# Attention and expert kernel on one core: Newton step of the norms moved to GpSimd, a layer norm's last step to ScalarE, and a new order of the calls

## Chip, cores and metric

One core of a Trainium2 chip. The time is the device time of one execution of the whole kernel in microseconds; the median of the runs counts, lower is better.

## What is computed

32 blocks of 128 tokens with 256 features each, and a context of the same shape. First a cross attention per block with 16 heads of 16 columns, whose scores are not divided by a constant but by the squared sum of the lengths of query and key:

```python
x = x + xattn(layernorm(x), ctx, ctx)
    # scores = alpha * 4 * (q.k) / (|q| + |k|)**2, softmax, times v, times Wo + bo
x = x + ffn(layernorm(x))
    # router softmax over 8 experts, best 2, weights renormalised
    # expert: gelu(x @ W1 + b1) @ W2 + b2, hidden size 1024
```

`layernorm(x) = (x - mean) / sqrt(var + 1e-5)`, without a learned scale.

## The kernel before, in words

**Two stages.** The attention stage works on 16 pairs of blocks (`NP`, index p or `it`, with b = 0 or 1 for the block in the pair). In it, the router picks two experts per token and scatters each token's record to a table in HBM, and the expert weights are split into two f16 halves, one matrix a pair. The expert stage (from L714 on) runs 71 slots of 128 records through the experts' two products and adds the results to the output. It is not touched by the change.

**Order.** Each engine has one instruction stream, written by hand-ordered calls: a loop over `it` with one call per step, each for pair it+2 down to it-3 (L328 SyncE, L589 TensorE, L873 ScalarE, L1270 VectorE, L1498 GpSimd). Nothing else orders the work but semaphores: an engine that waits in one call holds all calls behind it. In PSUM, scores (`s_ps`), factors (`u_ps`) and attention values (`pv_ps`) have places of their own, once each; 32 other uses a pair share three banks `gen` in a fixed cyclic order, the list `TURNS`. A use waits until the use three places earlier has been read.

**One pair's way through the attention stage.**
1. `means` (VectorE, L1048 to L1050): statistics of the input block. `norm` (GpSimd): the power -0.5 of the variance (L1435), then (x - mean) * rstd on 128x256 (L1439), into `xn`. TensorE transposes it (L404), ScalarE copies it out (L779, `x_turned`).
2. `project` (TensorE, L413 to L422): query, key and value. ScalarE `squares` (L794, L797) and `v_out` (L786). VectorE `squares` (L1067): the squared lengths `n2` of the 32 query and key heads of each block. ScalarE `roots`: y = exp(-0.5 ln n2) (L806, L808).
3. `norms` (VectorE, L1072 to L1087): one Newton step that makes the lengths exact, and their split into three bf16 parts in `ar`. TensorE `rows` (L433) transposes them; VectorE `rows` (L1095, L1098) copies them out; six DMAs of the SyncE queue (L307, `flat_rows`) lay them flat into `uk`.
4. GpSimd `units` (L1482, L1485) scales query and key; TensorE `stack` (L452, L459) transposes them, ScalarE `stack` (L814, L817) copies them out.
5. For n = 0 to 3 (block n // 2, half of the heads n % 2): TensorE `factors` (L474) sums the lengths by one matmul, ScalarE `factors` takes ln and exp of -2 times it (L825, L827). TensorE `scores` (L486); VectorE `scores`: product `tw` (L1108) and maxima `tm` (L1113). GpSimd `split_max`: for even n the maxima as two bf16 (L1466, L1468), for odd n subtracted from all scores (L1461). TensorE `turned` (L496, L504) transposes and, for even n, subtracts the maxima; ScalarE `turned` (L835) takes the exponential; TensorE `values` (L521).
6. `heads_out`, `heads_back`, `turn_on`, `o_turned`, `project_out`, `residual` (L842, L529, L1120, L1124, L536, L848, L543, L546, L1135): division by the sum, output projection and residual, stored by SyncE. Then the second layer norm `norm_again` (L1447, L1453), `turn_y` (L553), `record_high` and `record_low` (L855, L859, L1473), `logits` (L560, L1143).
7. Routing, for four blocks together, so every second pair: `choose`, `counts` in one iteration, `route_exp`, `shares` (L1178 on), `ranks` (L566), `positions` (L1200 to L1210) in another, then eight scatters from GpSimd (L1495). In pair 11's `positions` a table of the first 20 slots is made (`soon_tables`, L1230 on; its last row is that of L1227).
8. Weights: `weight_products` (L581), `weight_sum`, their exponent on VectorE, `weight_high` (ScalarE, L870), `weight_low` (VectorE, L1258).

The lines that the change moves to GpSimd:

```python
step(dve.tensor_tensor(na["y2"][:, :, :], na["y"][:, :, :], na["y"][:, :, :], ALU.mult))
step(dve.scalar_tensor_tensor(na["n2y2"][:, :, :], n2[:, :, :], TINY, na["y2"][:, :, :],
                              ALU.max, ALU.mult))
```

Of the kernel before, what the change touches and what calls it, by code (L numbers as in the profile page):

```python
# [78 lines left out]
def build(nc, ctx, io):  # L79
# [119 lines left out]
    with ExitStack() as a:  # L199
# [26 lines left out]
        norm_bufs = {"ln": stats(a, "ln")}  # L226
        qk = alloc(a, "qk", [P, 2, 2 * NH, DK], F32)
# [5 lines left out]
              for k in ("ln", "y", "y2", "n2y2", "rn", "r1", "r2")}  # L233
# [36 lines left out]
        def sync_program(sp):  # L270
# [57 lines left out]
            for it in range(-4, NP + 1):  # L328
                if 0 <= it < NP:
                    load_weights(it)  # L330
                if NE <= it - 1 < NP - 1:
                    store_w2(it - 1)
                if 0 <= it + 1 < NP:
                    flat_rows(it + 1)
# [4 lines left out]
                if 0 <= it < NP:  # L339
                    residual(1, it)  # L340
                if 2 <= it + 3 < NP:
                    load(1, it + 3)
                if 0 <= it - 1 < NP - 1:
                    store_x1(1, it - 1)
                if 2 <= it + 4 < NP:
                    load(0, it + 4)
                if it == -4:
# [49 lines left out]
        def tensor_program(pe):  # L397
# [191 lines left out]
            for it in range(-1, NP + 3):  # L589
                if 0 <= it - 2 < NP - 1:  # L590
                    logits(0, it - 2)
                if 0 <= it < NP:
                    stack(0, it)
                if 0 <= it - 1 < NP:
                    values(1, it - 1)
                    turned(2, 0, it - 1)
                if 0 <= it + 1 < NP:
                    norm(1, it + 1)
                if 0 <= it - 1 < NP:
                    weight_products(it - 1)  # L600
                    heads_back(0, it - 1)
                if 0 <= it - 2 < NP - 1:
                    turn_y(1, it - 2)
                if 0 <= it < NP:
                    factors(0, it)
                if 0 <= it - 2 < NP - 1:
                    logits(1, it - 2)
                if 0 <= it - 1 < NP:
                    weight_sum(it - 1)
                    turned(2, 1, it - 1)  # L610
                    turn_on(0, it - 1)
                if 0 <= it < NP:
                    scores(0, it)
                    stack(1, it)
                if 0 <= it - 3 < NP - 1 and it % 2 == 0:
                    ranks(it - 3)
                if 0 <= it < NP:
                    factors(1, it)
                if 0 <= it - 1 < NP - 1:
                    project_out(0, it - 1)  # L620
                if 0 <= it - 1 < NP:
                    turned(3, 0, it - 1)
                    values(2, it - 1)
                    turned(3, 1, it - 1)
# [990 lines left out]
```

## Time and profile before

| | us |
|---|---|
| median of 3 runs | 940.22 |
| lowest, highest | 936.03, 941.43 |
| the profiled execution's own time | 935.94 |
| its span, first to last instruction | 934.1 |
| TensorE, VectorE, ScalarE, GpSimd busy | 873.3, 686.2, 595.9, 450.2 |
| mean granted TensorE clock | 0.978 of full |

PE is TensorE, PEld its weight loads, DVE VectorE, ACT ScalarE, POOL GpSimd. Times in a timeline are microseconds from the span's start. "[0.28 <-DVE ar L1087]" behind a row says that the engine stood idle for 0.28 us before it and was released by that instruction. A busy time of TensorE holds modelled ends, so that neighbouring rows overlap; the distance from start to start says how long a group really holds the engine.

### The profile page before, as it was taken

To read this page: it belongs to the slowest core of one execution; us is meant where nothing else is said; L and a number is where in the kernel's file an instruction comes from. 1 tells how busy PE (TensorE), PEld (TensorE's weight loads), DVE (VectorE), ACT (ScalarE), POOL (GpSimd) and SP (SyncE) were. 2 spreads that over 40 slices of the span, in tenths; PEclk is the share of its full clock that TensorE was granted. 3 is DMA by queue.
4 is the path that set the end of the run, shared out by engine and by line. 5 is a ranking of instruction groups with operands and counts; after the bars stand their busy time and mean duration, and the time that the engine had idled before them with its cause. 6 is when DMAs were issued, how large, how long until landed. Compare 5 with 4: busy or idle time off the path is not lost.

```text
span 934.1 us, 29246 instructions
## 1 busy us (share of the span) xinstructions
PE 873.3 (93%) x10189; PEld 757.7 (81%) x10189; DVE 686.2 (73%) x1671; ACT 595.9 (64%) x1204; POOL 450.2 (48%) x508
## 2 busy tenths in 40 slices
PE   3899999999999999999887899999999999999994
PEld 2677887777777877777665798999999999999993
DVE  6677888888888888888767478666666666666662
ACT  2588887877878878788564464455555555555551
POOL 7445576758666586675554425323222322223222
PEclk9899999999999999999889899999999999999997
DMA  5212322223231453242344933432332323333322
GB/s 157 69 44 74 93 93 87 68 90 128 76 104 60 137 173 121 88 152 84 121 138 134 413 80 74 99 69 49 51 51 48 54 48 53 48 54 50 46 27 22
DMA packets 61885, 84.72 MB, mean 91 GB/s; under 512 B 9872, under 2 KB 55312, under 8 KB 59568
## 3 DMA queue, kind: packets, MB, share of 16 engines
q1 hardware_dynamic: 47504, 64.26, 21.8%
q0 software_dynamic: 13296, 18.00, 11.6%
q8 instruction: 86, 1.41, 0.6%
q10 hardware_dynamic: 944, 0.60, 0.2%
q14 instruction: 55, 0.45, 0.2%
HBM read 49.86 MB, written 31.92 MB: 88 GB/s over the span
## 4 chain that ended last, share of the span: by engine, by line
PE 75%; DVE 11%; issue 7%; ACT 2%; POOL 2%; DMA 1%; SPq 0%; DVEq 0%; POOLq 0%; ACTq 0%
PE s_ps L714 11%; PE pv_ps L732 10%; PE u_ps L714 10%; PE gen L732 10%; PE s_ps L486 5%; PE gen L496 4%; PE pv_ps L521 3%; PE gen L546 2%; PE gen L459 2%; PE gen L560 2%; PE u_ps L474 2%; PE gen L683 2%; PE gen L504 2%; PE gen L581 1%; DVE tw L1108 1%
## 5 line engine op out<-in xcount | busy, mean ns | idle before, releaser
L1542 POOL DMA_INDIRECT out<-yw,rb x71 | 110.4, 1554 | 268.3 <-DVE yw L1367 243.0
L937 ACT ACTIVATE h<-s_ps,b1t,inv 128x128 f32<-128x128 f32 x288 | 107.3, 458 | 89.6 <-PE s_ps L714 86.2
L937 ACT ACTIVATE h<-u_ps,b1t,inv 128x128 f32<-128x128 f32 x280 | 104.2, 460 | 87.2 <-PE u_ps L714 86.9
L1350 DVE TENSOR_SCALAR hs<-h,hsc 128x512 f16<-128x512 f32 x142 | 70.4, 496 | 120.5 <-ACT h L937 78.9
L835 ACT ACTIVATE pt<-gen,escale 128x512 f32<-128x512 f32 x128 | 87.0, 681 | 44.3 <-PE gen L504 35.4
L1352 DVE SCALAR_TENSOR_TENSOR hs<-h,hsc,hs 128x512 f16<-128x512 f32 x142 | 106.7, 751 | 5.1
L714 PE MATMUL s_ps<-xt,w1s 128*128 128x128 f16 x1728 | 105.3, 221 | 2.6 <-issue 2.5
L714 PEld LDWEIGHTS s_ps<-xt,w1s 128*128 x1728 | 100.4, 99 | 3.5 <-issue 3.0
L1495 POOL DMA_INDIRECT xrec<-rec,idx x64 | 72.3, 1129 | 62.3 <-DVE idx L1210 47.0
L714 PE MATMUL u_ps<-xt,w1s 128*128 128x128 f16 x1680 | 100.7, 219 | 1.4 <-issue 1.4
L732 PE MATMUL pv_ps<-w2s_sb,hs 128*128 x864 | 100.5, 272 | 0.9 <-issue 0.9
L714 PEld LDWEIGHTS u_ps<-xt,w1s 128*128 x1680 | 95.8, 98 | 2.1 <-issue 1.8
L732 PE MATMUL gen<-w2s_sb,hs 128*128 x840 | 97.4, 273 | 0.0
L1108 DVE TENSOR_TENSOR tw<-th,s_ps 128x1024 f32<-128x1024 f32 x64 | 77.8, 1216 | 21.9 <-PE s_ps L486 15.0
L732 PEld LDWEIGHTS pv_ps<-w2s_sb,hs 128*128 128x128 f16 x864 | 82.4, 98 | 11.2 <-issue 1.8
L732 PEld LDWEIGHTS gen<-w2s_sb,hs 128*128 128x128 f16 x840 | 80.8, 98 | 8.8
L496 PE MATMUL gen<-idf,tw 128*128 128x128 f32 x512 | 80.8, 281 | 1.3 <-ACT pt L835 0.6
L1113 DVE TENSOR_REDUCE tm<-tw 128x8 f32<-128x1024 f32 x64 | 78.1, 1220 | 2.2
L486 PE MATMUL s_ps<-kt,qt 32*128 32x128 f32 x1024 | 76.0, 287 | 0.7 <-DVE tw L1108 0.6
L1461 POOL TENSOR_TENSOR tw<-tw,tm 128x1024 f32<-128x1024 f32 x32 | 60.7, 1896 | 31.1 <-DVE tm L1113 31.1
L486 PEld LDWEIGHTS s_ps<-kt,qt 32*128 32x128 f32 x1024 | 63.6, 190 | 13.4 <-issue 11.8
L496 PEld LDWEIGHTS gen<-idf,tw 128*128 128x128 f32 x512 | 60.9, 145 | 15.9 <-issue 10.5
(241 smaller groups left out, 1684.0 us busy)
## 6 DMA issues: line engine op xcount, KB each, us to landing
wl<-L_ffn_W SPq DMA_DIRECT2D x16, 1024.0 KB
rb<-xrec SPq DMA_DIRECT2D x71, 132.5 KB
w2s<-wst SPq DMA_DIRECT2D x8, 1024.0 KB, 8.8
w2s_sb<-w2s SPq DMA_DIRECT2D x8, 1024.0 KB, 19.5
xin<-x SPq DMA_DIRECT2D x32, 128.0 KB, 2.1
cin<-ctx SPq DMA_DIRECT2D x32, 128.0 KB, 2.3
xres<-x SPq DMA_DIRECT2D x32, 128.0 KB, 2.5
out<-x SPq DMA_DIRECT2D x30, 128.0 KB, 2.1
```

Source lines behind the costliest of these rows:

```text
L486: ins = pe.matmul(s_ps[:, i, j * P:(j + 1) * P], qt[b][rws, j // 2, :], kt[b][rws, j // 2, j % 2, :], start=True, stop=True)
L496: ins = pe.matmul(g[:, j * P:(j + 1) * P], tw[h][:, i, j, :], idf[:, :], is_transpose=True, start=(j == 0), stop=(h == 1 and j == 3))
L714: ins = pe.matmul(hbank[n % HBANKS][:, o:o + SLOT], w, xt[s % 2][:, xp, k, :], start=(t == 0), stop=(t == len(terms) - 1))
L732: ins = pe.matmul(y, hs[s % 3][:, hp, m, :], w, start=(m == 0 and t == 0), stop=(m == HC - 1 and t == 2))
L835: act.activation(pt[n % 2][:, i, :], turn(f"ex{n}{i}", p)[:, :], ACT.Exp, scale=escale[:, :]).then_inc(sig(f"ex{n}{i}"), 1)
L937: ins = act.activation(h32[n % HBANKS][:, m % HB, :], hbank[n % HBANKS][:, o:o + SLOT], ACT.Gelu, scale=inv1[:, bass.ds(ex, 1)].bitcast(F3 ...
L1108: dve.tensor_tensor(tw[h][:, :, :, :].rearrange("p i j k -> p (i j k)"), th[h][:, :], s_ps[:, :, :].rearrange("p i k -> p (i k)"), ALU.mul ...
L1113: dve.tensor_reduce(tm[h][:, :], tw[h][:, :, :, :].rearrange("p i j k -> p (i j) k"), AX.X, ALU.max).then_inc(sig(f"tm{n}"), 1)
L1350: dve.tensor_scalar(hi, h, scale, None, ALU.mult).then_inc(sig("hi"), 1)
L1352: dve.scalar_tensor_tensor(lo, h, scale, hi, ALU.mult, ALU.subtract).then_inc(sig("lo"), 1)
L1495: pool.indirect_dma_start(xrec_d[:, :], bass.IndirectOffsetOnAxis(ap=idx[:, i, t:t + 1], axis=0), rec[m % 2][:, t, :], None).then_inc(sig( ...
L1542: pool.indirect_dma_start(out[:, :], bass.IndirectOffsetOnAxis(ap=rb[j][:, D + NE:D + NE + 1], axis=0), yw[s % 2][:, :], None, compute_op= ...
```

## The change

Five things change.

`norms` goes from VectorE's list to GpSimd's. There the steps with two operations on three operands are written as two instructions, or once for all (`n2c`), so nine become eleven. The layer norm's GpSimd part makes only a column `minus_mean` = -mean * rstd; ScalarE then writes `xn` by one activation with scale and bias. `TURNS` and the five lists of calls are put in a new order.

```diff
-    ("lg0", -2, "rl_0", None), ("qte0", 0, "qte0", None), ("kte0", 0, "kte0", None), ("ex20", -1, "ex20", None),
-    ("xct1", 1, "xce1", None), ("wgr", -1, "wdg", None), ("ob0", -1, "on", 0), ("xu1", -2, "xue", 1),
-    ("lg1", -2, "rl_1", None), ("wsum", -1, "wcl", None), ("ex21", -1, "ex21", None), ("oc0", -1, "ote", 0),
-    ("qte1", 0, "qte1", None), ("kte1", 0, "kte1", None), ("rank", -3, "rpos", None), ("wo0", -1, "x10", None),
-    ("ex30", -1, "ex30", None), ("ex31", -1, "ex31", None), ("qk1", 1, "qke1", None), ("v1", 1, "ve1", None),
-    ("xct0", 1, "xce0", None), ("qk0", 1, "qke0", None), ("v0", 1, "ve0", None), ("ex00", 0, "ex00", None),
-    ("ex01", 0, "ex01", None), ("ob1", -1, "on", 1), ("ex10", 0, "ex10", None), ("rows_t", 1, "rowq", None),
-    ("oc1", -1, "ote", 1), ("ex11", 0, "ex11", None), ("xu0", -1, "xue", 0), ("wo1", -1, "x11", None),
+    ("wo1", -2, "x11", None), ("ex10", -1, "ex10", None), ("ex11", -1, "ex11", None), ("ex20", -1, "ex20", None),
+    ("qte1", 0, "qte1", None), ("kte1", 0, "kte1", None), ("ex21", -1, "ex21", None), ("rows_t", 0, "rowq", None),
+    ("wgr", -1, "wdg", None), ("xu0", -2, "xue", 0), ("wsum", -1, "wcl", None), ("xu1", -2, "xue", 1),
+    ("lg0", -2, "rl_0", None), ("ob0", -1, "on", 0), ("lg1", -2, "rl_1", None), ("xct1", 1, "xce1", None),
+    ("xct0", 1, "xce0", None), ("ex30", -1, "ex30", None), ("rank", -3, "rpos", None), ("ex31", -1, "ex31", None),
+    ("qk1", 1, "qke1", None), ("v1", 1, "ve1", None), ("qk0", 1, "qke0", None), ("v0", 1, "ve0", None),
+    ("oc0", -1, "ote", 0), ("ob1", -1, "on", 1), ("ex00", 0, "ex00", None), ("wo0", -1, "x10", None),
+    ("oc1", -1, "ote", 1), ("ex01", 0, "ex01", None), ("qte0", 1, "qte0", None), ("kte0", 1, "kte0", None),
...
+        minus_mean = pair(a, "minus_mean", [P, 1], F32)
...
-              for k in ("ln", "y", "y2", "n2y2", "rn", "r1", "r2")}
+              for k in ("ln", "y", "n2c", "y2", "n2y2", "rn", "r1", "r2")}
...
+            def normed(b, p):
+                act.wait_ge(*at(f"sh{b}", p + 1))
+                if p:
+                    act.wait_ge(*at(f"xct{b}", p))
+                act.activation(xn[b][:, :], xin[b][:, :], ACT.Identity, bias=minus_mean[b][:, :],
+                               scale=norm_bufs["ln"][b][3][:, :]).then_inc(sig(f"xn{b}"), 1)
...
-            def norms(p):
-
-                dve.wait_ge(*at("ny", p + 1))
-                step(dve.tensor_tensor(na["y2"][:, :, :], na["y"][:, :, :], na["y"][:, :, :], ALU.mult))
-                step(dve.scalar_tensor_tensor(na["n2y2"][:, :, :], n2[:, :, :], TINY, na["y2"][:, :, :],
-                                              ALU.max, ALU.mult))
-                step(dve.scalar_tensor_tensor(na["rn"][:, :, :], na["n2y2"][:, :, :], -3.0, na["y"][:, :, :],
-                                              ALU.add, ALU.mult))
-                step(dve.scalar_tensor_tensor(na["r1"][:, :, :], n2[:, :, :], TINY, na["rn"][:, :, :],
-                                              ALU.max, ALU.mult))
-                if p:
-                    dve.wait_ge(*at("rows_t", p))
-                part = lambda i: ar[:, :, :, i * STRIP:i * STRIP + NH]
-                v4 = lambda t: t[:, :, :].rearrange("p b (i h) -> p b i h", h=NH)
-                step(dve.tensor_copy(part(0), v4(na["r1"])))
-                step(dve.tensor_tensor(v4(na["r2"]), v4(na["r1"]), part(0), ALU.subtract))
-                step(dve.tensor_copy(part(1), v4(na["r2"])))
-                step(dve.tensor_tensor(v4(na["r1"]), v4(na["r2"]), part(1), ALU.subtract))
-                dve.tensor_copy(part(2), v4(na["r1"])).then_inc(sig("parts"), 1)
...
+            steps = 0
+
+            def step(ins):
+                nonlocal steps
+                steps += 1
+                ins.then_inc(sig("pool_own"), 1)
+                pool.wait_ge(sig("pool_own"), steps)
...
             def norm(b, p):
                 _, mv, var, rstd = norm_bufs["ln"][b]
                 pool.wait_ge(*at(f"ln{b}ve", p + 1))
+                if p:
+                    pool.wait_ge(*at(f"xn{b}", p))
                 pool.tensor_tensor(rstd[:, :], var[:, :], mhalf[:, :], ALU.pow).then_inc(sig(f"ln{b}rs"), 1)
                 pool.wait_ge(*at(f"ln{b}rs", p + 1))
-                if p:
-                    pool.wait_ge(*at(f"xct{b}", p))
-                pool.tensor_scalar(xn[b][:, :], xin[b][:, :], mv[:, 0:1], rstd[:, :], ALU.subtract,
-                                   ALU.mult).then_inc(sig(f"xn{b}"), 1)
+                pool.tensor_scalar(minus_mean[b][:, :], rstd[:, :], mv[:, 0:1], -1.0, ALU.mult,
+                                   ALU.mult).then_inc(sig(f"sh{b}"), 1)
...
+            def norms(p):
+
+                for b in range(2):
+                    pool.wait_ge(*at(f"n2{b}", p + 1))
+                step(pool.tensor_scalar(na["n2c"][:, :, :], n2[:, :, :], TINY, None, ALU.max))
+                pool.wait_ge(*at("ny", p + 1))
+                step(pool.tensor_tensor(na["y2"][:, :, :], na["y"][:, :, :], na["y"][:, :, :], ALU.mult))
+                step(pool.tensor_tensor(na["n2y2"][:, :, :], na["n2c"][:, :, :], na["y2"][:, :, :], ALU.mult))
+                step(pool.tensor_scalar(na["n2y2"][:, :, :], na["n2y2"][:, :, :], -3.0, None, ALU.add))
+                step(pool.tensor_tensor(na["rn"][:, :, :], na["n2y2"][:, :, :], na["y"][:, :, :], ALU.mult))
+                step(pool.tensor_tensor(na["r1"][:, :, :], na["n2c"][:, :, :], na["rn"][:, :, :], ALU.mult))
+                if p:
+                    pool.wait_ge(*at("rows_t", p))
+                part = lambda i: ar[:, :, :, i * STRIP:i * STRIP + NH]
+                v4 = lambda t: t[:, :, :].rearrange("p b (i h) -> p b i h", h=NH)
+                step(pool.tensor_copy(part(0), v4(na["r1"])))
+                step(pool.tensor_tensor(v4(na["r2"]), v4(na["r1"]), part(0), ALU.subtract))
+                step(pool.tensor_copy(part(1), v4(na["r2"])))
+                step(pool.tensor_tensor(v4(na["r1"]), v4(na["r2"]), part(1), ALU.subtract))
+                pool.tensor_copy(part(2), v4(na["r1"])).then_inc(sig("parts"), 1)
...
```

The lists, one iteration each (numbers in brackets are n or b; n,i for `turned`; the offset of the pair against `it` where it is not 0):

TensorE before: logits(0) -2, stack(0), values(1) -1, turned(2,0) -1, norm(1) +1, weight_products -1, heads_back(0) -1, turn_y(1) -2, factors(0), logits(1) -2, weight_sum -1, turned(2,1) -1, turn_on(0) -1, scores(0), stack(1), ranks -3, factors(1), project_out(0) -1, turned(3,0) -1, values(2) -1, turned(3,1) -1, project(1) +1, factors(2), values(3) -1, norm(0) +1, scores(1), project(0) +1, turned(0,0), scores(2), factors(3), turned(0,1), heads_back(1) -1, turned(1,0), rows +1, values(0), turn_on(1) -1, turned(1,1), turn_y(0) -1, project_out(1) -1, scores(3).

TensorE after: factors(3) -1, project_out(1) -2, turned(1,0) -1, turned(1,1) -1, scores(3) -1, values(0) -1, turned(2,0) -1, stack(1), turned(2,1) -1, rows, weight_products -1, turn_y(0) -2, values(1) -1, weight_sum -1, turn_y(1) -2, logits(0) -2, heads_back(0) -1, values(2) -1, logits(1) -2, norm(1) +1, norm(0) +1, scores(0), turned(3,0) -1, ranks -3, turned(3,1) -1, factors(0), project(1) +1, values(3) -1, factors(1), project(0) +1, scores(1), turn_on(0) -1, factors(2), heads_back(1) -1, turned(0,0), project_out(0) -1, scores(2), turn_on(1) -1, turned(0,1), stack(0) +1.

ScalarE after: turned(1,0) -1, normed(1) +1, turned(1,1) -1, turned(2,0) -1, stack(1), turned(2,1) -1, record_high(0) -2, heads_out(0) -1, record_high(1) -2, weight_high -1, x_turned(0) +1, x_turned(1) +1, normed(0) +2, turned(3,0) -1, turned(3,1) -1, factors(0), squares(1) +1, v_out(1) +1, factors(1), route_exp -2, squares(0) +1, heads_out(1) -1, v_out(0) +1, o_turned(0) -1, factors(2), turned(0,0), roots +1, o_turned(1) -1, turned(0,1), stack(0) +1, factors(3).

VectorE before: scores(1) -1, squares(1), squares(0), means(1) +1, norms, heads_back(1) -2, rows, scores(2) -1, residual(1) -2, logits(0) -2, scores(3) -1, weight_diagonal -1, heads_back(0) -1, means(0) +2, logits(1) -2, weight_exponent -1, shares and positions -3 (even it) or choose and counts -2 (odd it), residual(0) -1, weight_low -1, scores(0).

VectorE after: scores(1) -1, heads_back(1) -2, squares(0), residual(0) -2, scores(2) -1, residual(1) -2, scores(3) -1, means(0) +2, rows, weight_diagonal -1, weight_exponent -1, logits(0) -2, heads_back(0) -1, logits(1) -2, shares and positions -3 (even it) or choose -2 (odd it), weight_low -1, counts -2 (odd it), means(1) +2, scores(0), squares(1) +1.

GpSimd after: norm(1) +2, record_low(0) -2, units(1) +1, split_max(0), units(0) +1, split_max(1), norms +1, split_max(2), norm_again(0) -1, norm_again(1) -1, norm(0) +3, split_max(3), five scatters -3 (even it), record_low(1) -1, three scatters -2 (odd it). Before, three scatters of -4 (odd it) or three of -3 (even it) stood behind split_max(3), and two of -3 (even it) behind split_max(1).

SyncE after: flat_rows, store_w2 -1, load(0) +3, load_weights, load(1) +3, residual(1), store_x1(1) -1, residual(0), store_x1(0) -1. Before: load_weights, store_w2 -1, flat_rows +1, residual(0), store_x1(0) -1, residual(1), load(1) +3, store_x1(1) -1, load(0) +4.

The calls behind the attention loop, among them the last pair's output projection and routing, are as before.

## Rows read from the trace of the kernel before

**Rows 1.** Page, part 1: busy us (share of the span) xinstructions.

```profile
PE 873.3 (93%) x10189; PEld 757.7 (81%) x10189; DVE 686.2 (73%) x1671; ACT 595.9 (64%) x1204; POOL 450.2 (48%) x508
```

**Rows 2.** Timeline of PE: start us, us, engine line op; weight products, first expert product.

```profile
51.01 1.08 PE L581 MATMUL gen<-wl 128*128 128x128 bf16 x16
...
137.03 1.08 PE L581 MATMUL gen<-wl 128*128 128x128 bf16 x16
...
432.94 1.08 PE L581 MATMUL gen<-wl 128*128 128x128 bf16 x16
...
469.19 1.08 PE L581 MATMUL gen<-wl 128*128 128x128 bf16 x16
...
517.01 4.58 PE L714 MATMUL s_ps<-xt,w1s 128*128 128x128 f16 x48 [2.51 <-issue]
```

**Rows 3.** Windows: stretch, length, busy PE PEld DVE ACT POOL, clock, DMA, GB/s.

```profile
80.00:110.00 30.00, 29.58 (x311) 24.15 (x308) 23.11 (x52) 24.20 (x42) 18.14 (x23) 1.00 0.27 82
...
137.00:433.00 296.00, 288.26 (x2994) 232.56 (x2993) 256.70 (x671) 237.27 (x396) 204.17 (x261) 1.00 0.34 109
...
440.00:500.00 60.00, 52.37 (x503) 41.35 (x502) 44.09 (x108) 37.80 (x58) 30.60 (x37) 0.86 0.33 109
```

**Rows 4.** Timeline of PE inside one pair.

```profile
305.40 0.60 PE L496 MATMUL gen<-idf,tw 128*128 128x128 f32 x4
305.84 0.61 PE L504 MATMUL gen<-negb,mhl 128*128 128x128 bf16 x8
...
306.73 0.60 PE L496 MATMUL gen<-idf,tw 128*128 128x128 f32 x4
307.62 0.42 PE L433 MATMUL gen<-idb,ar 128*96 128x128 bf16 x4 [0.28 <-DVE ar L1087]
```

**Rows 5.** Waits, 137 to 433 us: engine line <- releaser: us, times, longest.

```profile
POOL xrec L1495 <- DVE idx L1210: 30.0, 5, 6.1
ACT pt L835 <- PE gen L504: 20.5, 26, 1.6
...
PE gen L433 <- DVE ar L1087: 3.5, 10, 0.4
...
PE gen L504 <- POOL mhl L1468: 1.8, 5, 0.4
```

**Rows 6.** Timeline of DVE: first of the nine norm instructions, one inside, the row behind.

```profile
304.61 0.22 DVE L1072 TENSOR_TENSOR na_y<-na_y 128x64 f32<-128x64 f32 x1
...
306.74 0.59 DVE L1086 TENSOR_TENSOR na_r<-na_r,ar 128x64 f32<-128x64 f32 x1
...
307.48 0.25 DVE L1120 RECIPROCAL rz<-gen 128x16 f32<-128x16 f32 x1
```

**Rows 7.** Groups of POOL: busy us, mean ns of one; idle before.

```profile
L1439 POOL TENSOR_SCALAR xn<-xin,ln_mv,ln_rstd 128x256 f32<-128x256 f32 x32 | 40.5, 1264 | 12.7 <-PE gen L404 10.0
...
L1482 POOL TENSOR_TENSOR qu<-qk,colscale 128x256 f32<-128x256 f32 x32 | 19.7, 616 | 0.0
...
L1466 POOL CAST mhl<-tm 128x8 bf16<-128x8 f32 x32 | 6.0, 188 | 30.3 <-DVE tm L1113 30.3
```

**Rows 8.** Groups of ACT.

```profile
L855 ACT ACTIVATE rec<-xn 128x256 f16<-128x256 f32 x32 | 13.3, 416 | 0.0
```

**Rows 9.** Timeline of PE: behind the early tables, and in the last pair.

```profile
446.43 0.59 PE L413 MATMUL gen<-bqp,ones_b 96*128 96x512 bf16 x1 [4.02 <-DVE x L1135]
...
480.82 0.60 PE L474 MATMUL u_ps<-uk,aq 99*128 99x512 bf16 x2 [1.99 <-ACT th L825]
```

**Rows 10.** Timeline of PE at the start.

```profile
24.23 0.66 PE L433 MATMUL gen<-idb,ar 128*96 128x128 bf16 x4 [4.25 <-DVE ar L1087]
```

**Rows 11.** Timelines of DVE and POOL.

```profile
87.98 2.34 DVE L1258 SCALAR_TENSOR_TENSOR w1s<-wl,wsc,w1s 128x2048 f16<-128x2048 f32 x1
...
88.14 2.60 POOL L1447 TENSOR_TENSOR lm_rstd<-lm_var,mhalf 128x1 f32<-128x1 f32 x1 [6.48 <-DVE lm_var L1050]
```

**Rows 12.** Groups of POOL: scatters.

```profile
L1495 POOL DMA_INDIRECT xrec<-rec,idx x64 | 72.3, 1129 | 62.3 <-DVE idx L1210 47.0 <-issue 15.3
```

More of the change, by code:

```diff
@@ L338, in sync_program @@
                     store_x1(0, it - 1)
[L339 to L347, printed above, removed]
+                if it == -3:
                     sp.wait_ge(*at("set_pool", 4))
@@ L589, in tensor_program @@
             for it in range(-1, NP + 3):
+                if 0 <= it - 1 < NP:
+                    factors(3, it - 1)
                 if 0 <= it - 2 < NP - 1:
-                    logits(0, it - 2)
-                if 0 <= it < NP:
-                    stack(0, it)
+                    project_out(1, it - 2)
+                if 0 <= it - 1 < NP:
+                    turned(1, 0, it - 1)
+                    turned(1, 1, it - 1)
+                    scores(3, it - 1)
+                    values(0, it - 1)
+                    turned(2, 0, it - 1)
@@ L594, in tensor_program @@
+                if 0 <= it < NP:
+                    stack(1, it)
+                if 0 <= it - 1 < NP:
+                    turned(2, 1, it - 1)
+                if 0 <= it < NP:
+                    rows(it)
+                if 0 <= it - 1 < NP:
+                    weight_products(it - 1)
+                if 0 <= it - 2 < NP - 1:
+                    turn_y(0, it - 2)
                 if 0 <= it - 1 < NP:
                     values(1, it - 1)
-                    turned(2, 0, it - 1)
+                    weight_sum(it - 1)
@@ L597, in tensor_program @@
+                if 0 <= it - 2 < NP - 1:
+                    turn_y(1, it - 2)
+                    logits(0, it - 2)
+                if 0 <= it - 1 < NP:
+                    heads_back(0, it - 1)
+                    values(2, it - 1)
+                if 0 <= it - 2 < NP - 1:
+                    logits(1, it - 2)
                 if 0 <= it + 1 < NP:
                     norm(1, it + 1)
+                    norm(0, it + 1)
+                if 0 <= it < NP:
+                    scores(0, it)
@@ L608, in tensor_program @@
                 if 0 <= it - 1 < NP:
[L609 to L616, printed above, removed]
+                    values(3, it - 1)
                 if 0 <= it < NP:
                     factors(1, it)
-                if 0 <= it - 1 < NP - 1:
-                    project_out(0, it - 1)
@@ L621, in tensor_program @@
[L621 to L624, printed above, removed]
-                if 0 <= it + 1 < NP:
-                    project(1, it + 1)
-                if 0 <= it < NP:
-                    factors(2, it)
-                if 0 <= it - 1 < NP:
-                    values(3, it - 1)
-                if 0 <= it + 1 < NP:
-                    norm(0, it + 1)
-                if 0 <= it < NP:
-                    scores(1, it)
@@ L637, in tensor_program @@
                 if 0 <= it < NP:
-                    turned(0, 0, it)
-                    scores(2, it)
-                    factors(3, it)
-                    turned(0, 1, it)
+                    scores(1, it)
+                if 0 <= it - 1 < NP:
+                    turn_on(0, it - 1)
+                if 0 <= it < NP:
+                    factors(2, it)
                 if 0 <= it - 1 < NP - 1:
@@ L644, in tensor_program @@
                 if 0 <= it < NP:
-                    turned(1, 0, it)
-                if 0 <= it + 1 < NP:
-                    rows(it + 1)
+                    turned(0, 0, it)
+                if 0 <= it - 1 < NP - 1:
+                    project_out(0, it - 1)
                 if 0 <= it < NP:
-                    values(0, it)
+                    scores(2, it)
                 if 0 <= it - 1 < NP - 1:
@@ L1282, in vector_program @@
                 if 0 <= it < NP:
-                    rows(it)
+                    squares(0, it)
+                if 0 <= it - 2 < NP - 1:
+                    residual(0, it - 2)
                 if 0 <= it - 1 < NP:
```

191 lines of the change are left out of this document (103 added, 88 removed).

## The prediction

> **What bounds the kernel now.** I read the page first, then windows, the waits of the middle stretch, and the timelines. The page gives TensorE as the busiest engine, 93% of the span [rows 1]. The change touches the attention stage alone. That stage ends at 517.01 us, when the expert stage's first product starts [rows 2]; from there on the code is the same, so I carry 417 us over unchanged.
>
> The stage's beat is read from the weight product of each pair. From the pair at 137.03 to that at 432.94 lie ten pairs, 29.59 us each; the three pairs before, from 51.01, took 28.67 each; 432.94 to 469.19 took 36.25 [rows 2]. In the ten, TensorE is busy 288.3 of 296 us at full clock, VectorE 256.7, ScalarE 237.3, GpSimd 204.2 [rows 3]. Busy TensorE is not TensorE at its peak: the row after the transposes L496 starts 0.44 us later when nothing holds it (305.40 to 305.84), but 0.89 us later where the norm rows come next (306.73 to 307.62) [rows 4]. Taking every kind of group of TensorE's timeline at its shortest distance from start to start, as here, one pair of the stretch adds up to 27.4 us. So 2.2 us of every beat is waiting, and 27.4 is the floor: the change takes no matmul away.
>
> Who makes it wait? The waits show TensorE held by VectorE's last norm instruction, 3.5 us in ten pairs and once in each, and by GpSimd's split maxima, 1.8 us [rows 5]; the rest is spread in pieces under 0.3 us. VectorE itself is the near bound: 25.7 busy plus some 1 us between dependent instructions leaves under 3 of 29.6. The three quick pairs are a natural experiment: most of the routing on VectorE starts only behind them, VectorE is busy for 23.1 of 30 us there, against 26.0 later [rows 3], and the beat is 0.9 us shorter.
>
> **The change, part by part.**
>
> *Newton step and split of the norms leave VectorE.* Nine instructions from 304.61 to 307.48 go: 2.9 us a pair [rows 6]. That brings VectorE to the load of the quick pairs.
>
> *They arrive on GpSimd* as eleven, each behind a semaphore. The trace has no such form there. Below: 11 of the small 128x8 cast's kind, 0.19, plus 0.08 between, 3 us. Above: 11 of the 128x256 multiply's kind, 0.62 and 0.08, 7.7 us [rows 7]. 64 columns lie a quarter of the way between 8 and 256, so I take 0.3 and 0.08, 4.2 us. Their cover is slack: the square roots on ScalarE now come after the third factor exponential, while the row transposes on TensorE moved from just before values(0) to the eighth place of the next iteration. Counting TensorE's order at its shortest distances, the roots are ready at 25.5 us of an iteration and the rows wanted 6.4 into the next, at 33.8; GpSimd is free for the norms at 25.9 to 26.6. So the rows wait for nothing up to 7 us. The cover is thinner for what is queued behind: split_max(2), 0.45 us, whose result TensorE wants at 31.8. With 4.2 it is done at 30.6 to 31.3; beyond 4.7 turned(2,0) is late by the rest, every pair.
>
> *First layer norm.* GpSimd loses two 1.26 us instructions and gains two on one column (0.2, as the small cast, to 0.6, as the multiply; I take 0.25): minus 2.0 [rows 7]. ScalarE gains two 128x256 activations, 0.42 each as its copy of the same size, 0.3 when pipelined: 0.6 to 0.8 a pair on 23.7 busy [rows 3, 8]. GpSimd in sum gains 2.2 us a pair on 20.4; ScalarE and GpSimd stay under 25 of 27.4. The input tile is now freed by ScalarE, so the SyncE queue waits for it there. Walked through, its order is: row copies, input, weights, other input, residuals, stores; the wait of the second input ends about 3 us before the next row copies can go. I cost it at nothing; its cover is that gap.
>
> *The new order* is the larger part. I laid the new TensorE list out at its shortest distances and put VectorE, ScalarE and GpSimd beside it with the durations of their rows. The 31 or 32 uses of the three shared PSUM banks find their bank free, the tightest by 0.1 to 0.5 us (turned(2,1) behind ScalarE's exponential of turned(2,0), misses by 0.2). VectorE finishes tw of scores(0) about 1.7 us before scores(1) wants the bank. So the list closes near 27.6. Between that and 29.59 I take 28.4: just below the quick pairs' 28.67, since the load is theirs and the wait for the norms is gone besides, a full microsecond above the floor, since the old order stays 1.3 to 2.2 above it too. Ten pairs: minus 11.9; the three quick ones, minus 0.3 each: minus 0.9. Bounds: 0 and minus 22.
>
> *The pair with the early tables.* VectorE works on them, and TensorE waits 4.02 us for the residual behind [rows 9]; its next matmuls run at half clock. With the same in the last pair, the granted clock is 0.86 of full over 440 to 500: 8.4 us of full clock lost, some 3.4 of it here [rows 3]. In the new order the tables lie before the weights' low half and scores(0); with 1.7 us of slack about 3 us of wait remain, and much of the clock loss. Minus 1.5, bounds minus 7 and plus 3.
>
> *The last pair* waits 1.99 us, with no projections to fill in [rows 9], and then loses the other 5 us to the clock. The new order has the same want of filling; VectorE's lighter load gives minus 1, bounds minus 6 and plus 4. Its tail, from the last scores on VectorE to the first product, is VectorE's own list and hardly changed.
>
> *Start.* First rows on TensorE come at 24.23, behind the norms, which ran beside GpSimd's units [rows 10]. Now GpSimd does the units first and the norms after them, to about 25.6: plus 1, bounds minus 1 and plus 5.
>
> Sum: -11.9 - 0.9 - 1.5 - 1 + 1 = -14.3. The profiled execution took 935.94 us (span 934.1), so it would be 922. The median of the runs shown is 940.22, 4.3 above it; my forecast is for such a median: **926 us**.
>
> **A rule against the change.** While VectorE runs its weight split of 2.34 us (from 87.98), GpSimd's power on one column, begun at 88.14, takes 2.60 us [rows 11], for one column, where the whole multiply of 128x256 takes 0.62 [rows 7]; and of the norm instructions L1086 takes 0.59 where its like L1072 takes 0.22 [rows 6]. So each engine is held while the other has something they share. The Trainium skill, "SBUF — State Buffer", section "Who interferes with whom", says why: the two share one port pair under an exclusive lock, and a VectorE instruction with two SBUF inputs, or in a two-port mode, blocks a GpSimd one that reads SBUF. The trace agrees. In the new order the norms on GpSimd meet VectorE's work from PSUM and its reductions, whose neighbours on GpSimd show no such stretch; the weight split meets the scatters, as it did before. By my sum this costs the path nothing.
>
> **The rivals.**
>
> *R1, the GpSimd queue becomes the wait (slower).* In every second iteration its first three scatters stand before the next pair's statistics, units and split maxima, and they wait for idx, which VectorE writes about 14.3 us into TensorE's list. They cost 1.13 us each and a gap of 0.24 [rows 12]; one is held by the weight split for 1.3 more. Then statistics, record, units and split_max(0) follow: I get 23.6, and TensorE wants the maxima at 23.0. The other place is split_max(2) behind the norms. With the norms near the upper bound, 7.2 us, 3.0 over my price, turned(2,0) stalls for about 2 us in each of 14 pairs: -14.3 + 28 = plus 14, so **954**. It decides from 0.5 to 1.2 us over my price per pair, and cancels the gain from 2 us. For it: GpSimd waited 30 us for idx, five times in ten pairs, even before [rows 5]. Against: none of these reached TensorE. 0.16.
>
> *R2, it moves VectorE's load but the beat stays.* TensorE and ScalarE take turns through single score and factor banks, and 20.5 us of ScalarE's exponentials waited on TensorE [rows 5]. If that coupling sets 29.6, only small terms are left: **938**. Against: the quick pairs. 0.16.
>
> *R3, the order closes at the floor*, 27.6: 13 pairs give minus 22 to minus 24 in sum: **916**. For it: the layout above. Against: the quickest pairs shown took 28.67. 0.18.
>
> *R4, the new order stalls longer in the two special pairs* and the clock halves for longer, as it did after 1.99 us [rows 9]: both at their bad end, 4.5 and 5 above my terms: about **935**, 0.05.
>
> Forecast: 0.45. **Range 912 to 944**, leaving out most of R1 and the tail of R3. A measurement of this kernel can tell 0.5%, 4.7 us, from no change: faster 0.68 (forecast, R3, R4), same 0.16 (R2), slower 0.16 (R1).
>
> **What would show it.** In the changed profile: a beat of 28.4 between weight products (R2: 29.5; R3: 27.6; R1: over 30, uneven from pair to pair); VectorE near 23 us a pair; the eleven norm instructions on GpSimd in 4.2 us; no wait of the row transposes for them; after the early tables, TensorE waiting for tw instead of x. I am wrong if L504 waits for mhl by more than 1 us a pair, or row transposes wait for GpSimd.

## The result and the profile after

The changed kernel took **956.36 us** (median of 4, 955.88 to 956.92), the kernel before 938.65 beside it (median of 4): ratio **1.0187**, 95% interval 1.016 to 1.0215. The forecast was 926 with a range of 912 to 944. The prediction was wrong, and in its sign.

The page of the changed kernel, part 1 (span 954.8 us), against [rows 1]:

```profile
PE 882.6 (92%) x10189; PEld 766.1 (80%) x10189; DVE 653.5 (68%) x1527; ACT 611.6 (64%) x1236; POOL 453.3 (47%) x684
```

VectorE lost 33 us of work, ScalarE gained 16. GpSimd's gain is only 3: the norms (53.3) and the bias columns (8.6) came, the two 1.26 us instructions a pair (40.5) went, and its powers on one column (L1435 and L1447 before, L1444 and L1454 now), which took up to 2.60 us beside VectorE's work [rows 11], fell from 50.7 to 36.3 us in sum.

The windows of the changed kernel, cut at its weight products (L582; 203.73, 232.31 and 265.89), with [rows 3]'s columns:

```profile
203.73:232.31 28.58, 28.46 (x303) 23.17 (x302) 22.63 (x58) 24.42 (x42) 20.64 (x37) 1.00 0.30 94
232.31:265.89 33.58, 31.27 (x301) 25.02 (x300) 23.78 (x58) 24.84 (x43) 21.28 (x39) 0.90 0.25 78
...
137.00:433.00 296.00, 281.31 (x2852) 227.11 (x2853) 221.73 (x563) 233.56 (x393) 199.83 (x346) 0.96 0.33 104
```

Pairs take turns: 28.6 us, near the 28.4 forecast, then 33 to 35. From 168.67 on the stretches are 35.1, 28.6, 33.6, 28.6, 32.9, 28.6, 32.9, 28.6, 32.9, then 35.6 with the early tables and 32.4 for the last. The first four are 27.8 to 28.7. In the long ones the clock is 0.90, in the short ones 1.00.

What happens at the start of a long one? The timeline of the changed kernel from 235.11, GpSimd's, TensorE's, VectorE's and ScalarE's rows (in brackets the idle time before, and who ended it):

```profile
235.11 1.12 POOL L1523 DMA_INDIRECT xrec<-rec,idx  x1 [0.17 <-issue]
...
235.59 0.65 PE L522 MATMUL pv_ps<-pt,vz 128*32 128x128 f32 x16
...
236.16 0.61 PE L561 MATMUL gen<-wr_sb,xn2t 128*128 128x8 f32 x4
...
236.54 0.96 POOL L1523 DMA_INDIRECT xrec<-rec,idx  x1 [0.30 <-issue]
236.63 0.63 PE L405 MATMUL gen<-idf,xn 128*128 128x128 f32 x4
...
239.46 0.17 DVE L1140 TENSOR_SCALAR r_l<-gen 128x8 f32<-128x8 f32 x1 [3.04 <-remote]
...
239.77 1.09 PE L497 MATMUL gen<-idf,tw 128*128 128x128 f32 x4 [1.42 <-DVE r_l L1140]
...
240.92 0.66 ACT L790 ACTIVATE xct<-gen 128x256 f32<-128x256 f32 x2 [3.38 <-remote]
...
241.64 1.12 PE L497 MATMUL gen<-idf,tw 128*128 128x128 f32 x4 [0.78 <-ACT xct L790]
```

The logits matmul L561 stands at 236.16, and VectorE, which waits for it alone, gets it at 239.46. The norm transposes L405 stand at 236.63, and ScalarE gets them at 240.92. TensorE's own rows hardly show a gap; its results come some 3 us late. Then its next groups wait for the banks that VectorE and ScalarE hold, and the clock falls (windows of the same kernel):

```profile
232.31:239.50 7.19, 6.04 (x89) 4.91 (x87) 2.65 (x13) 4.54 (x7) 6.01 (x7) 1.00 0.30 91
239.50:246.40 6.90, 5.85 (x18) 4.24 (x19) 6.25 (x21) 4.38 (x7) 2.14 (x3) 0.51 0.22 70
```

Beside it stand the five scatters that GpSimd issues back to back in every second iteration (five rows L1523, 235.11 to 240.34). In the waits from 137 to 433 these late results are two groups that the kernel before has not:

```profile
ACT xct L790 <- remote: 17.6, 5, 4.2
DVE r_l L1140 <- remote: 15.2, 5, 3.1
```

To compare traces I counted the matmuls that signal a semaphore and whose signal comes over 0.6 us behind their start, from 130 to 440 us: 41 in the changed kernel, **46 in the kernel before**, near scatters but for a few of 0.65 us in the changed kernel. There they had been hidden in the beat of 29.6. Such a signal is called late below. (Where a record is missing the next signal is read. Such single readings, logits(0) in five pairs, are in the 41. Where I say none, they are left out, and so are readings of 0.65 us beside no scatter: seven in a_order_only, one in a_five_later.)

### The profile page after: what moved, and what is told of

Read it like the earlier page. It is cut to its first block, busy times and chain, and to the rows that moved or that the text cites. A ratio compares the mean times of both kernels' runs of the same rounds, so it can differ in the third digit from the quotient of the medians.

```text
span 954.8 us, 29371 instructions
## 1 busy us (share of the span) xinstructions
PE 882.6 (92%) x10189; PEld 766.1 (80%) x10189; DVE 653.5 (68%) x1527; ACT 611.6 (64%) x1236; POOL 453.3 (47%) x684
## 4 chain that ended last, share of the span: by engine, by line
PE 80%; DVE 4%; issue 4%; ACT 3%; DMA 3%; SPq 2%; another core or an unknown queue 2%; POOL 1%; DVEq 0%; POOLq 0%; ACTq 0%
PE pv_ps L736 9%; PE gen L736 9%; PE u_ps L718 9%; PE s_ps L718 9%; PE s_ps L487 6%; PE gen L497 6%; PE pv_ps L522 3%; PE u_ps L475 3%; PE gen L505 3%; PE gen L416 3%; PE gen L547 3%; PE gen L419 3%; PE gen L423 2%; DMA w2s_sb<-w2s 2%
## 5 line engine op out<-in xcount | busy, mean ns | idle before, releaser
L954 ACT ACTIVATE h<-u_ps,b1t,inv 128x128 f32<-128x128 f32 x280 | 104.5, 460 | 84.4 <-PE u_ps L718 84.3
L1523 POOL DMA_INDIRECT xrec<-rec,idx x64 | 72.0, 1125 | 58.8 <-DVE idx L1207 42.7
L497 PEld LDWEIGHTS gen<-idf,tw 128*128 128x128 f32 x512 | 59.3, 146 | 27.8 <-issue 12.7
```

The lines of the kernel that those rows point to most:

```text
L497: ins = pe.matmul(g[:, j * P:(j + 1) * P], tw[h][:, i, j, :], idf[:, :], is_transpose=True, start=(j == 0), stop=(h == 1 and j == 3))
L954: ins = act.activation(h32[n % HBANKS][:, m % HB, :], hbank[n % HBANKS][:, o:o + SLOT], ACT.Gelu, scale=inv1[:, bass.ds(ex, 1)].bitcast(F3 ...
L1523: pool.indirect_dma_start(xrec_d[:, :], bass.IndirectOffsetOnAxis(ap=idx[:, i, t:t + 1], axis=0), rec[m % 2][:, t, :], None).then_inc(sig( ...
```

## The experiments

Three theories, T1 to T3, were to be told apart. T1: scatters make TensorE's results late; five back to back, where no bank is to spare, turn that into a stall. T2: TensorE's instruction loads do it; a load of 16 KB at 236.29 falls into the stall, and one stretch of two pairs holds five loads, so the phase stays. T3: the new order has no slack there, whatever the scatters do. Kernels that were measured together ran on one chip, whose number is given; that of the first measurement is not known.

**Chip 0.** *a_spread*: two of the five scatters stay, one goes behind split_max(0) and two behind units(0) of the next iteration.

```
-scatter(1,1) (2,0) (2,1) (3,0) (3,1)   behind split_max(3), it even
+scatter(1,1) (2,0)                     behind split_max(3), it even
+scatter(2,1)                           behind split_max(0), it odd
+scatter(3,0) (3,1)                     behind units(0), it odd
```

> The changed kernel with the five scatters that GpSimd starts back to back (L1523, 235.11 to 241.30 in its trace) split into 2, 1 and 2: two stay after the last split_max, one stands behind split_max(0) and two behind units(0) of the next iteration, where GpSimd has 2.1 us of idle time. T1 (scatters back to back, under way while the banks of TensorE have no slack, hold up its completions, and the clock gate adds to it): the stretches of 32.9 to 35 us between weight products fall to 29 to 31, and the time to 930 to 943. T2 (the stall comes from TensorE's instruction loads, which fall at the same phase): the long stretches stay, 952 to 958. T3 (the new order alone has no slack at that place): the same, 952 to 960.

928.34 us, before 930.37; ratio 0.9983 (0.9957 to 1.001). Long stretches 29.5.

*a_five_later*: all five behind split_max(0), it odd.

> The changed kernel with all five scatters moved together, still back to back, to behind split_max(0) of the next iteration (249.9 in its trace instead of 235.1). T1: a stall still comes every second pair, but some 15 us after the place it has now (the reads of values and scores at weight product + 3 to + 10 us run on time, and split_max(1) and the norms come 4 to 6 us late instead): 940 to 965. T2 and T3: the stall at weight product + 3 us stays where it is, in addition to the delay of the norms: 960 to 990.

940.08; ratio 1.0116 (1.008 to 1.0151). Long stretches 31.5, with no late signal: with split_max(1), the units and the norms queued behind them, five scatters at this place cost 3 us by GpSimd's queue alone.

*b_five*: the kernel before, `scatter(1,1)` and `(2,0)` moved to the head of its group of three.

> The kernel before with the grouping of the changed one: the scatters (1,1) and (2,0), which it starts at the end of an iteration, are put in front of the three behind split_max(3), so that five stand back to back. T1 in its strong form (five back to back stall TensorE wherever they are): 2 to 4 us more in every second pair, 950 to 965. T1 with bank slack as the condition: 940 to 948. T2 and T3: no change but the 2.5 us that GpSimd's next calls come later, 937 to 942.

930.11; ratio 1.0009 (0.9984 to 1.0034).

*a_shift*: `for _ in range(64): pe.transpose(g[:, 0:P], idf, idf)` ahead of TensorE's first wait for xn.

> The changed kernel with 64 more transposes of the identity at the very start of TensorE's program, while it waits for the first x: 128 instructions more in front of everything, about half of one instruction load. T2: the loads move by some 13 us against the work, the stalls of 3 to 5 us at weight product + 3 us vanish or move to another place of the pair, and the time changes by 5 us or more. T1 and T3: the long stretches stay at 32.9 to 35 us at the same place, and the time is that of the changed kernel within 4 us, 953 to 960.

926.58; ratio 0.9965 (0.9947 to 0.9983), every stretch of the middle 28.4 or 28.6. This looked like T2. It lacked a control: the changed kernel itself on that chip. None of the four traces of chip 0 has a late signal, so that none of these runs can judge T1 to T3.

**Chip 15** gave it. *a_again* is the changed kernel unaltered; *a_shift16*, *a_shift32* and *a_shift128* put 16, 32 and 128 transposes ahead, the last a whole load.

> The changed kernel, unaltered, on the chip and beside the runs of the kernel before that the other kernels have. If the stall belongs to the program: 1.8 to 2.1% slower than before again, long stretches of 32.9 to 35 us in every second pair. If it belongs to the chip or the session it was measured on (T5): no long stretches, and the time of a_shift, 0.3% under before.

> 16 more transposes at the start of TensorE's program, 32 instructions more in front of everything. T2 (place of TensorE's instruction loads decides): loads come some 1 to 3 us earlier against the work, the stall shrinks or moves; 926 to 950. T1 or T3 with the start's timing as the trigger: as a_shift, 927. T5: 927.

> 32 more transposes, 64 instructions more in front of everything, a quarter of a load. T2: in between a_shift16 and a_shift, 926 to 940. Other theories: as a_shift, 927.

> 128 more transposes, 256 instructions more in front of everything, which is one whole load of 16 KB, so the loads fall at the same instructions of the loop as in the changed kernel. T2: the stalls come back, long stretches of 32.9 us, 950 to 962. If a_shift is faster for any other reason (TensorE busy before the first x, a later start), this one is as fast or up to 5 us slower: 926 to 933.

a_again **925.98**, before 930.53; ratio **0.9942** (0.9923 to 0.9962). The shifts gave 925.94 (0.9949), 926.65 (0.9953) and 926.87 (0.9959, 0.9938 to 0.998). So the stall is not in the program alone, and nothing shows that the shift healed anything. Windows of a_again at the same two pairs, then the middle stretch:

```profile
196.50:225.10 28.60, 28.48 (x304) 23.20 (x303) 22.62 (x58) 24.55 (x41) 20.66 (x37) 1.00 0.32 99
225.10:253.60 28.50, 28.38 (x302) 23.21 (x300) 24.07 (x58) 24.66 (x43) 22.77 (x39) 1.00 0.30 93
137.00:433.00 296.00, 294.68 (x3126) 241.10 (x3124) 240.49 (x613) 254.25 (x430) 221.41 (x375) 1.00 0.35 111
```

and its timeline at the place of the stall:

```profile
227.94 1.12 POOL L1523 DMA_INDIRECT xrec<-rec,idx  x1 [0.17 <-issue]
...
228.99 0.61 PE L561 MATMUL gen<-wr_sb,xn2t 128*128 128x8 f32 x4
...
229.63 0.17 DVE L1140 TENSOR_SCALAR r_l<-gen 128x8 f32<-128x8 f32 x1 [0.40 <-PE gen L561]
...
230.26 0.65 ACT L790 ACTIVATE xct<-gen 128x256 f32<-128x256 f32 x2
...
231.11 1.09 PE L497 MATMUL gen<-idf,tw 128*128 128x128 f32 x8
```

The same five scatters, 2.8 us behind the weight product as in the first trace; VectorE waits 0.40 us for the logits, not 3.04. TensorE's instruction load falls here too, at 228.74, 3.6 us behind the weight product (4.0 in the first trace), and nothing is late: a load at this place does not make the stall by itself.

**Chip 14**: both kernels again, and two parts of the change.

> The kernel before, unaltered, for its trace on the chip on which the others run. It should show its beat here: if the 0.9% that separates its median here (930) from the first session's (938.65) is one of waits in the pairs, the stretches between weight products are under 29.6 us here; if they are 29.6 again, the difference lies outside them. Ratio 1.00.

> The changed kernel, unaltered, once more. If the 1.9% of the first session belongs to one chip or one session, this comes out at 0.994 of before again (925 to 927) on any chip but that one; if it comes and goes with the load of the program, some sessions show 1.019. A trace with long stretches would show whether the five scatters stand beside them.

b_again 930.5 (0.998, 0.9962 to 0.9999) and a_again2 **927.3**, before 931.76; ratio **0.995** (0.993 to 0.9969). The kernel before has no late signal here, and its beat is 29.3 (29.6 and 28.9 in turn), where it was 29.59 [rows 2]. b_again and the kernel before beside it are the same program, and 0.998 is what they differ by: 0.2% is not to be read as a gain here. So in the first trace every second pair of the kernel before had hidden 0.6 us of the same trouble.

*a_norms_dve*: the changed kernel with the norms back on VectorE, as before the change, behind residual(0).

> The changed kernel with its new order, but the eleven instructions of the norms back on VectorE (ten there, behind residual(0)). My account of the gain (VectorE freed of 2.8 us in a pair, and the rows no longer late): the beat goes back from 28.45 to 29 or more, 931 to 938. Rival (the new order gives all of it, VectorE has slack with it): the beat stays at 28.3 to 28.6, 922 to 928, and the start is some 3 us shorter.

929.8; ratio 0.9982 (0.9963 to 1.0002). The beat is the rival's: the stretches stay at 28.4 to 28.6, two at 29.1. The time lies between the two forecasts (922 to 928, 931 to 938), and the start is not shorter: the first weight product stands at 57.02, in a_again2 at 56.61. Its window shows VectorE nearly as loaded as before ([rows 3] has 256.70), with TensorE waiting hardly at all:

```profile
137.00:433.00 296.00, 293.70 (x3127) 240.20 (x3126) 253.07 (x692) 254.04 (x429) 192.22 (x268) 1.00 0.35 111
```

*a_order_only*: in addition, GpSimd does the whole first normalisation again (`xn <- xin, mv, rstd`), at the places where it now computes the bias.

> The new order of calls alone: norms on VectorE, the first layer norm's normalisation on GpSimd (1.23 us twice in a pair instead of 0.26 twice, and 0.4 us less twice for ScalarE). If both moves matter: beat 29.2 to 30, 933 to 945. If the order gives the gain: 28.3 to 28.7, 922 to 929.

985.72; ratio 1.0575 (1.0547 to 1.0603), stretches 32.3 to 34.9, far outside both forecasts. Its waits from 190 to 440:

```profile
POOL mhl L1484 <- DVE tm L1119: 34.6, 7, 5.0
POOL xn L1457 <- PE gen L405: 30.4, 8, 4.2
...
PE gen L497 <- POOL tw L1479: 18.0, 8, 2.3
```

GpSimd may write xn only when TensorE has turned the last one. It waits for that up to 4.2 us at the head of its queue, and split_max is late behind it. On ScalarE that wait has no such followers.

**Chip 4**: the unaltered kernels once more, in search of the conditions of the first measurement.

> The changed kernel, unaltered, once more. As in a_again and a_again2: 925 to 928, 0.993 to 0.997 of before, no completions of TensorE late beside scatters. As in the first measurement: 955 to 957, 1.016 to 1.021, stalls of 2.7 us from weight product + 3 us on.

> The changed kernel with its five scatters split into 2, 1 and 2. Where the changed kernel takes 926: 926 to 930, no better than it. Where it takes 956: T1 gives 930 to 942, T3 gives 952 or more.

> The kernel before, for its trace. As in b_again: beat of 29.2 (29.6 and 28.9 in turn) and no completion of TensorE late by over 0.6 us. As in the first trace: beat 29.6 and over 40 late completions.

They were there again. a_again3 **959.36**, before 936.37; ratio **1.0238** (1.0221 to 1.0255). a_spread2 **937.08**; ratio 1.0001 (0.9988 to 1.0014). b_again2 936.51 in one run, with 47 late signals; the changed kernel has 42, and ScalarE waits up to 5.01 us for one of them (at 180.04). Windows of a_again3 and of a_spread2, short and long stretch:

```profile
205.50:234.10 28.60, 28.48 (x304) 23.19 (x302) 22.63 (x58) 24.43 (x41) 20.71 (x37) 1.00 0.29 90
234.10:267.60 33.50, 31.23 (x302) 25.05 (x300) 23.83 (x58) 24.87 (x42) 21.34 (x39) 0.90 0.24 78
```

```profile
198.00:226.60 28.60, 28.48 (x305) 23.22 (x303) 22.64 (x58) 24.44 (x41) 21.92 (x38) 1.00 0.28 84
226.60:256.80 30.20, 28.69 (x301) 23.07 (x300) 23.15 (x58) 24.63 (x42) 20.26 (x38) 1.00 0.32 101
```

TensorE's program is the same in both, to the instruction, and a load stands near the start of the stall in both (237.75 and 230.63, 3.6 and 4.0 us behind the weight product). Three scatters moved on GpSimd take 22 us away, the clock stays at 1.00, and VectorE's wait for the logits, late by 3.04 us above, is 1.64 in a_spread2, so signals are still late there:

```profile
232.40 0.17 DVE L1140 TENSOR_SCALAR r_l<-gen 128x8 f32<-128x8 f32 x1 [1.64 <-PE gen L561]
```

This is T1's forecast (930 to 942) and neither T2's (952 to 958, given for a_spread) nor T3's (952 or more).

*a_ln_pool*: the changed kernel with only the first normalisation back on GpSimd.

> The changed kernel, norms on GpSimd as in it, but the first layer norm's normalisation back on GpSimd (1.23 us twice in a pair, and its wait for TensorE's transposes at the head of GpSimd's queue). If that move is what the new order needs: stretches of 32 to 36 us and 980 to 1000 us, as in a_order_only or worse, since GpSimd also has the norms. Rival (it was VectorE's norms in a_order_only that broke the order): 926 to 935.

990.34; ratio 1.0568 (1.0549 to 1.0586): the rival falls. The wait of xn for TensorE (37.8 us, 8 times, from 190 to 440) is there with the norms on either engine.

**Chip 12.** *a_paced* was to move the five behind the scores.

```
+record_low(1, it - 1)
+if it < NP: pool.wait_ge(su0, it + 1)
 scatter(1,1) ... scatter(3,1)
-record_low(1, it - 1)
```

> The changed kernel with record_low(1) in front of the five scatters and a wait of GpSimd for scores(0) of the same iteration before them, so that they start some 3.4 us later, when TensorE has its stretch of small matmuls behind it; norm(1) comes up to 2 us later. Where before takes 936: if the place decides, stretches of 28.4 to 30 us and 928 to 938; if the number back to back decides wherever they stand, 31 to 34 us and 945 to 960. Where before takes 930: 925 to 930.

943.17, before 934.7; ratio 1.0082 (1.0056 to 1.0107); 41 late signals. The edit was not what it was meant to be: it waits for scores that TensorE has long done, and only record_low, now ahead, moves the scatters, by 1.0 us (3.8 us behind the weight product, not 2.8). Long stretches 31.0 to 31.9, but at full clock:

```profile
229.40:260.40 31.00, 28.87 (x301) 22.97 (x299) 23.41 (x58) 24.20 (x42) 23.45 (x39) 1.00 0.26 84
```

The long stretches are 2 to 5 us shorter than those of a_again3, which would give the place some weight; but the unaltered changed kernel was not measured on chip 12, so this compares across chips only.

*a_paced2* waits for `su0, it + 2`. It met **chip 11**.

> As a_paced, with the wait that was meant: GpSimd waits for scores(0) of the next pair (TensorE, weight product + 6 us) before the five scatters, so that they start some 3.4 us later than in the changed kernel and end after the time at which norm(1) is now ready; norm(1) and split_max(0) come up to 4 us later. Where before takes 934 or more: if the place decides, no completion of TensorE is late by over 1.5 us, stretches of 28.6 to 30.5 us and 928 to 938; if the number back to back decides wherever they stand, a stall of 2 us or more among the projections and 940 to 955. Where before takes 930: 926 to 934.

927.85, before 930.96; ratio 0.9964 (0.9941 to 0.9986), no late signal, long stretches 29.0. It costs nothing that the ratio can tell there, and says nothing about the other kind.

In sum, the seven measurements fall into two kinds. Chips 0, 15, 14, 11: before 930 to 932, the changed kernel (on 15 and 14) 0.994 and 0.995, no late signals. The first measurement and chips 4 and 12: before 935 to 939, 36 to 47 late signals in every trace but a_ln_pool's (24, of which ten are of 0.65 us), the changed kernel 1.019 (first) and 1.024 (chip 4).

## Why the prediction was wrong, by its own steps

**The step that failed** is in "The new order": TensorE's list laid out at its shortest distances, with banks "tightest by 0.1 to 0.5 us", and the scatters priced only in GpSimd's own time. In the rule against the change I wrote that the weight split meets the scatters as before and costs the path nothing. I never asked what a moved group of scatters does to TensorE. It went from 3, 3 and 2 to 3 and 5, placed 3 us behind the weight product. The trace of before had the warning in its 46 late signals, which no view of waits names, as the old order's slack took them but for some 0.6 us in every second pair. What the step missed, measured: a_again3's 33.5 to 35.8 us against 28.4 in five stretches, and in the first measurement the last pair's excess too, 32.4 against 28.4. Summed from 168.67 to 518.40 the first measurement is 30.6 us longer than a_again (25.3 in the five, 1.3 with the early tables, 3.9 in the last), of a difference in span of 34.0 (954.8 to 920.8). The clock, 0.51 over 6.90 us, takes up to 3.4 us of full-speed work behind each stall; I had counted that for the special pairs only. Shown by a_spread2 against a_again3 is that the five scatters as placed cost 22 us there; how they reach TensorE is not.

**No rival was it.** R1 had the right place (scatters, GpSimd), the right side and 954, but its mechanism is refuted: the waits of the changed kernel show neither L505 behind mhl by more than 0.3 us in ten pairs nor L434 behind the norms (only at the start it waits for them, see below). R2 to R4 were not seen.

**The beat.** 28.4 was right in every undisturbed stretch (28.6 in the short ones of the first measurement, 28.4 and 28.6 in turn in a_again). Its starting point was not: 29.59 was a disturbed value, and 29.3 is the undisturbed one. So where nothing is late the ten pairs give -7.6 us and not -11.9; the three quick ones give -1.6 (86.0 in b_again, 84.4 in a_again) for -0.9.

**Its reason** was half wrong. "The load is theirs and the wait for the norms is gone": a_norms_dve has VectorE at the old load and a beat of 28.5. The quick pairs were no experiment on load. The order gives the shorter beat, and needs ScalarE's normalisation, with the calls where they stand (a_order_only, a_ln_pool: 32 us and more without it). In time the parts are not told apart: without the norms' move the ratio is 0.9982 with an interval that holds 1, and the move itself gives 929.8 to 927.3, some 0.3%, with two intervals that touch. So about half of the 0.5% may be the norms' move after all: it saves 1.0 us in the pair with the early tables (35.4 to 34.4) and 0.5 and 0.7 in two others.

**The norms on GpSimd.** Forecast 0.3 each and 4.2 in all; measured 0.24 to 0.39 and 4.1 (25.95 to 30.06 at the start). The small bias instruction took 0.26 (0.25 forecast). These two were right:

```profile
L1486 POOL TENSOR_SCALAR na_n2c<-n 128x64 f32<-128x64 f32 x9 | 3.5, 387 | 0.0
...
L1501 POOL CAST ar<-na_r 128x64 bf16<-128x64 f32 x9 | 2.1, 236 | 0.6
```

Mis-sized was ScalarE's `xn`: 0.60 us each (L783), 1.2 a pair for a forecast of 0.6 to 0.8, which cost nothing that shows in the beat.

**The early tables.** Forecast: TensorE waits some 3 us, for tw instead of x. It waits 3.95 in the first measurement and in a_again:

```profile
468.91 2.08 PE L487 MATMUL s_ps<-kt,qt 32*128 32x128 f32 x16 [3.95 <-DVE tw L1105]
```

The pair takes 34.3 in a_again, 34.6 in b_again: -0.2 for a forecast of -1.5. **The last pair** gives 28.4 against 28.6, -0.2 for -1.

**Start.** The rows wait for GpSimd, which ends the norms at 30.06 and not at 25.6. The 25.6 was a wrong sum: in the trace of before GpSimd's units end at 25.37, and 4.2 us of norms behind them end at 29.6.

```profile
24.86 0.51 POOL L1485 COPY ku<-qk 128x128 f32<-128x128 f32 x2
```

In the changed kernel the rows on TensorE come 5.9 us later than at 24.23 [rows 10]:

```profile
30.12 0.66 PE L434 MATMUL gen<-idb,ar 128*96 128x128 bf16 x4 [1.26 <-POOL ar L1501]
```

The first weight product stands at 55.0 to 56.6 in four traces of the changed kernel, at 51.0 to 54.9 in four of the old order: some 3 us later, forecast +1, bound +5.

**The sum where nothing is late.** Pairs and start give about -7; the ratios 0.9942 and 0.995 on 931 give -5.4 and -4.7. The forecast had -14.3. That a_again's 925.98 is the number forecast is chance in part: before was 8 us lower there too.

## What to carry to other kernels

Before an order is packed tighter, compare each matmul's start with the moment its reader gets it, not only the waits: lateness that slack hides is the first thing the new order pays for. Moving a DMA issue on one engine, and how many stand in a row, is a change to every other engine. And a control of the unaltered kernel on the same chip comes before any fix: a_shift seemed to heal a stall that no trace of its chip has.

## What the hardware showed that I had not expected

This program has two kinds of measurement. In one, TensorE's signals come 0.7 to 5.5 us late near GpSimd's scatters; in the other none does, with the same instructions at the same distances. Every chip was measured at one time only, so that it is a property of the chip and not of the time is likely, not shown. How a scatter delays TensorE is open. It is not scatters alone: the three at 212.65 to 217.65 of the first trace, where TensorE has long matmuls, left nothing late. Whether the place or the number decides stays open as well, since a_paced2 met the wrong kind, and T2 is ruled out as the sole cause (a_spread2, a_again), not as a part. Nor is the new order's want of slack (T3) ruled out as a condition: five in a row in the old order (b_five) were measured only where nothing is late.

A scatter on GpSimd is longer beside VectorE's weight split in both kinds (2.47 us at 212.65 of the first trace too). In a_again:

```profile
232.45 2.35 DVE L1255 SCALAR_TENSOR_TENSOR w1s<-wl,wsc,w1s 128x2048 f16<-128x2048 f32 x1
...
233.16 2.47 POOL L1523 DMA_INDIRECT xrec<-rec,idx  x1 [0.30 <-issue]
```

2.47 us instead of 0.96.

The Trainium skill, "SBUF — State Buffer", section "Who interferes with whom", says that "PE and ACT never wait on anyone". The section is about the engines' SBUF ports. On which path a scatter and TensorE meet no run here shows, so for the ports the sentence is neither borne out nor refuted. Read for TensorE as a whole, the traces of chips 0, 15, 14 and 11 agree with it; those of the first measurement and of chips 4 and 12 do not, with TensorE's results up to 5.5 us late beside GpSimd's scatters, and there the measurement decides.
